# A fused attention, butterfly and linear-attention kernel: its semaphore waits rewritten, the instruction orders kept

## What is computed

```python
x = x + windowed_attention(_layernorm(x))    # 16 heads of 8, 2 key/value heads, window 32
x = x + butterfly_ffn(_layernorm(x))         # 128 -> 512, 9 butterfly stages, gelu, 9 stages, -> 128
x = x + linear_attention(_layernorm(x))      # elu+1 features, sum over all tokens of a batch
x = x + butterfly_ffn(_layernorm(x))
```

## Time and profile before

| | us |
|---|---|
| three executions | 560.13 (median), 557.11, 562.09 |
| span of the profiled execution | 560.6 |
| PE busy in it | 525.0 |
| DVE, POOL, ACT busy | 441.2, 450.9, 358.7 |

### The profile page before, as it was taken

How to read it: one execution, slowest core, us unless ns; L and a number is a source line. 1 busy time by engine, 2 the same in 40 slices (tenths; PEclk the granted TensorE clock), 3 DMA queues, 4 the chain that set the end, 5 groups by cost and what they waited for, 6 DMA issues and landing times. The chain is left out here.

```text
span 560.6 us, 14708 instructions
## 1 busy us (share of the span) xinstructions
PE 525.0 (94%) x5060; PEld 345.8 (62%) x5060; DVE 441.2 (79%) x1272; ACT 358.7 (64%) x578; POOL 450.9 (80%) x646
## 2 busy tenths in 40 slices
PE   5786998979999999999999999999999999999795
PEld 3442554546766666666667676666666667777563
DVE  5778789897888989898988898888989797663341
ACT  2543376567687767676777768686767777664532
POOL 6665689899898999999898989899999797955420
PEclk9789799989999999999999999999999999999899
DMA  9533232322223232232313231323232222100001
GB/s 310 170 76 81 63 83 54 81 74 56 54 58 80 62 76 66 68 78 48 102 45 87 63 87 44 84 60 77 61 76 50 59 66 58 39 1 20 1 20 37
DMA packets 49546, 38.88 MB, mean 69 GB/s; under 512 B 12352, under 2 KB 38976, under 8 KB 49472
## 3 DMA queue, kind: packets, MB, share of 16 engines
q1 hardware_dynamic: 47024, 33.73, 23.9%
q10 hardware_dynamic: 2448, 4.22, 2.1%
HBM read 15.64 MB, written 5.51 MB: 38 GB/s over the span
## 5 line engine op out<-in xcount | busy, mean ns | idle before, releaser
L501 POOL TENSOR_TENSOR probs_t<-probs_t,first 128x1024 f32<-128x1024 f32 x64 | 151.3, 2367 | 11.5 <-DMA probs_t<-probs_t 11.5
L645 PEld LDWEIGHTS ring<-w,early 128*128 128x128 f32 x1024 | 119.0, 192 | 9.6 <-issue 7.0
L982 ACT ACTIVATE early<-ring,b 128x512 f32<-128x512 f32 x128 | 87.2, 684 | 54.7 <-PE ring L633 53.1
L645 PE MATMUL ring<-w,early 128*128 128x128 f32 x1024 | 120.0, 275 | 0.8 <-ACT early L982 0.8
L972 ACT ACT_TABLE_LOAD x58 | 74.4, 1283 | 10.7 <-issue 9.7
L601 PE MATMUL ps_s<-kx,q_t 64*32 64x512 f32 x960 | 65.9, 606 | 3.4 <-DVE merged L1268 2.7
L633 PE MATMUL ring<-xT_G,w1b 128*128 128x512 f32 x128 | 67.1, 612 | 0.7 <-ACT xT_G L960 0.7
L991 ACT ACTIVATE probs_t<-merged_t 128x1024 f32<-128x1024 f32 x64 | 65.3, 1044 | 3.8 <-DVE merged_t L1275 3.7
L633 PE MATMUL ring<-xT_F,w1b 128*128 128x512 f32 x128 | 59.9, 611 | 0.4 <-ACT xT_F L960 0.4
L1255 DVE COPY_PREDICATED ps_s<-first,ps_s 128x512 f32<-128x512 uint32 x64 | 43.6, 681 | 9.2 <-PE ps_s L601 9.0
L1282 DVE STREAM_TRANSPOSE ps_o<-ps_o 128x512 f32<-128x512 f32 x64 | 46.2, 722 | 1.6 <-PE ps_o L618 0.3
(11 more groups left out here) (124 smaller groups left out, 1023.9 us busy)
## 6 DMA issues: line engine op xcount, KB each, us to landing
probs_t<-probs_t SPq DMA_DIRECT2D x256, 64.0 KB, 2.0
kx<-kv_rows SPq DMA_DIRECT2D x120, 40.0 KB, 2.2
x_P<-in_x SPq DMA_DIRECT2D x16, 256.0 KB, 3.2
out_x<-x_G SPq DMA_DIRECT2D x16, 256.0 KB, 2.4
vx_t<-kv_rows SPq DMA_DIRECT2D x128, 8.0 KB
up_s<-in_up_m ACTq DMA_DIRECT2D x7, 256.0 KB, 8.4
down_s<-in_down_m ACTq DMA_DIRECT2D x7, 256.0 KB, 8.4
kv_rows<-kv_t SPq DMA_DIRECT2D x16, 80.0 KB, 2.8
```

The costliest lines, as they stand in the source:

```text
L501: nc.gpsimd.tensor_tensor(parts, parts, keep.rearrange("p (a t) -> p a t", a=1).to_broadcast([P, PAIR * HEADS, WIN]), ALU.mult).then_inc(p ...
L645: last = nc.tensor.matmul(bank(name)[:, P * j:P * (j + 1)], hid[s][:, c, P * j:P * (j + 1)], w2[:, c], start=(c == 0), stop=(c == CH - 1))
L982: nc.scalar.activation(hid[s][:, c], bank(name)[:], ACT.Gelu, bias=b1[:, c:c + 1]).then_inc(drained[BANK[name]].sem, 1)
```

## The change

It rewrites the waits; what each engine does, and in which order, stays, but for six POOL instructions.

1. **Order of waits.** Wherever an operation has several waits, the one that is expected last is now written first, so that the operation itself carries it, and the early ones stand in the EVENT_SEMAPHORE.
2. **Two waits on one semaphore become one** (`both(...)`, the larger of the values). On ACT nearly every operation loses its EVENT_SEMAPHORE by this.
3. **`residual`** no longer ends with a wait for its own result; the wait stands at the head of `moments` instead. `head_outputs` and `linear_normalised` are split into one function per operation, called in the same order.
4. **POOL** drops `nm` and `nmr` where VectorE applies the norm itself (group 0 P, group 15 F and L), and the wait on the group before's `nmr`. The semaphore `pool_step` is called `rooted`.
5. **Bookkeeping.** The lags of all tables and turns are renumbered (`TURNS` from NG + 14 to NG + 7), runs of single pieces are put together; on PE, `W.PV0` now carries the wait on `parted` and `W.S0` the one on the keys' DMA.

The number of EVENT_SEMAPHORE instructions in the built program goes from 638 to 527 on DVE, from 355 to 79 on ACT, from 200 to 140 on POOL, from 248 to 251 on PE and from 65 to 63 on SP.

```diff
...
 class Count:
...
+    def both(self, *events):
+
+        return max(self.value(group, name) for group, name in events)
...
+            def rooted_variance(g, s, mean=None):
+                pool.wait_ge(vec.sem, vec.after(g, f"{s}.mv"))
+                nc.gpsimd.tensor_scalar(rv[s][:], mv[s][:, :, 1], LN_EPS, None, ALU.add).then_inc(rooted.sem, 1)
+                if mean is not None:
+                    nc.gpsimd.tensor_scalar(mean, mv[s][:, :, 0], -1.0, None, ALU.mult).then_inc(rooted.sem, 1)
+                pool.wait_ge(rooted.sem, rooted.after(g, f"{s}.rv"))
...
+                nc.gpsimd.tensor_tensor(rstd[s][:], rv[s][:], half[:], ALU.pow).then_inc(rooted.sem, 1)
+
             def normalise(g, s):
...
-                if (g == 0 and s == "P") or (g == NG - 1 and s in "FL"):
-                    return
+                rooted_variance(g, s, nm[s][:])
+                pool.wait_ge(rooted.sem, rooted.after(g, f"{s}.rstd"))
+                nc.gpsimd.tensor_tensor(nmr[s][:], nm[s][:], rstd[s][:], ALU.mult).then_inc(rooted.sem, 1)
+                pool.wait_ge(rooted.sem, rooted.after(g, f"{s}.nmr"))
                 pool.wait_ge(product.sem, product.after(g - 1, TURNED[s]))
-                pool.wait_ge(pool_step.sem, pool_step.after(g, f"{s}.nmr"))
...
             def copy_out(g, name, dst, *freed):
 
-                act.wait_ge(product.sem, product.after(g - 1, *freed))
-                act.wait_ge(product.sem, product.after(g, name))
+                act.wait_ge(product.sem, product.both((g, name), *((g - 1, user) for user in freed)))
...
             def probs_out(g, j):
                 ready(ACT.Exp)
 
+                act.wait_ge(vec.sem, vec.after(g, f"W.tr{j}"))
                 act.wait_ge(product.sem, product.after(g - 1, f"W.PV{j}"))
-                act.wait_ge(vec.sem, vec.after(g, f"W.tr{j}"))
...
             def residual(g, s, name, base):
 
+                dve.wait_ge(product.sem, product.after(g, name))
...
-                dve.wait_ge(biased.sem, biased.after(g, f"{base}.xb"))
-                dve.wait_ge(product.sem, product.after(g, name))
...
-                if s != "G":
-                    dve.wait_ge(own.sem, own.after(g, name))
...
             def row_max(g, j):
+                dve.wait_ge(vec.sem, vec.after(g, f"W.cp{j}"))
                 dve.wait_ge(drained["S"].sem, drained["S"].after(g - 1, f"W.S{j}"))
-                dve.wait_ge(vec.sem, vec.after(g, f"W.cp{j}"))
...
             def subtract_max(g, j):
-                dve.wait_ge(vec.sem, vec.after(g if j >= 2 else g - 1, f"W.tr{(j - 2) % 4}"))
-                dve.wait_ge(vec.sem, vec.after(g, f"W.max{j}"))
+                dve.wait_ge(vec.sem, vec.both((g, f"W.max{j}"), (g if j >= 2 else g - 1, f"W.tr{(j - 2) % 4}")))
...
```

More of the change, by code:

```diff
@@ L464, in add_bias @@
                         pool.wait_ge(bffn_made, 1)
-                behind = 2 if s == "P" else 1
-                pool.wait_ge(drained[BANK[used]].sem, drained[BANK[used]].after(g - behind, used))
                 if source is None:
@@ new lines, in turn @@
+                for g in due(t, 5):
+                    add_bias(g, "F", bproj_s, "F.down", "L.proj")
+                for g in due(t, 2, 2):
+                    add_bias(g, "P", bo_s, None, "W.proj")
+                for g in due(t, 4, 2):
+                    normalise(g, "W")
+                for g in due(t, 3, 0, 1):
+                    probs_parted(g, 2)
+                for g in due(t, 4, 0, 1):
+                    add_bias(g, "W", bffn_s, "W.proj", "F.down")
+                for g in due(t, 6, 0, 14):
+                    normalise(g, "L")
@@ new lines, in turn @@
+                for g in due(t, 3, 2):
+                    probs_parted(g, 2)
+                for g in due(t, 6):
+                    add_bias(g, "L", bffn_s, "L.proj", "G.down")
+                if t == 20:
+                    rooted_variance(15, "L")
+                for g in due(t, 4, 2):
+                    add_bias(g, "W", bffn_s, "W.proj", "F.down")
+                if t == 19:
+                    rooted_variance(15, "F")
+                for g in due(t, 3, 1):
+                    probs_parted(g, 3)
@@ L586, in scores @@
                 name = f"W.S{j}"
-                if j == 0:
-                    drained_by(g, "P.q", name)
-                    if g == 0:
-                        pe.wait_ge(early_cleared, 3)
-                        drained_by(0, "X.ka", name)
-                    else:
-                        pe.wait_ge(kx_in.sem, kx_in.after(g, "P.kx"))
-                if j == 2 and g == 0:
-                    drained_by(0, "X.kb", name)
+                if (name, "keys") not in COVERED and g > 0:
+                    pe.wait_ge(kx_in.sem, kx_in.after(g, "P.kx"))
+                drained_by(g, "P.q", name)
+                if g == 0:
+                    drained_by(0, "X.ka" if j < TPB else "X.kb", name)
+                    pe.wait_ge(early_cleared, 3)
                 free(g, name)
@@ L609, in weighted_values @@
                 name = f"W.PV{j}"
-                if j == 0:
+                pe.wait_ge(parted.sem, parted.after(g, f"W.um{j}"))
+                if (name, "values") not in COVERED:
                     pe.wait_ge(vec.sem, vec.after(g, "W.vx"))
-                pe.wait_ge(parted.sem, parted.after(g, f"W.um{j}"))
                 free(g, name)
@@ L779, in turn @@
-                for g in due(t, 7, 2, 15):
+                for g in due(t, 3, 2):
                     scores(g, 1)
+                if t == 5:
+                    weighted_values(1, 0)
+                    up_transposed()
+                    weighted_values(1, 1)
+                for g in due(t, 6):
+                    linear_kv_rows(g, 0)
+                    linear_q(g)
+                    linear_kv_rows(g, 1)
+                for g in due(t, 8, 0, 14):
+                    ffn_down(g, "G")
@@ new lines, in turn @@
+                for g in due(t, 5):
+                    norm_transposed(g, "F", "W")
+                for g in due(t, 3, 2):
+                    scores(g, 2)
+                for g in due(t, 4, 2):
+                    weighted_values(g, 1)
+                for g in due(t, 6):
+                    linear_state(g)
+                for g in due(t, 5):
+                    ffn_up(g, "F", 3)
+                    ffn_up(g, "F", 2)
+                    ffn_up(g, "F", 0)
+                    ffn_up(g, "F", 1)
@@ new lines, in turn @@
+                for g in due(t, 6, 0, 14):
+                    linear_out(g, 0)
+                for g in due(t, 7):
+                    norm_transposed(g, "G", "L")
+                if t == 21:
+                    linear_out(15, 0)
+                for g in due(t, 3, 1):
+                    scores(g, 3)
+                for g in due(t, 4):
+                    weighted_values(g, 2)
+                for g in due(t, 2, 2):
+                    attention_q(g)
+                for g in due(t, 5):
+                    ffn_down(g, "F")
@@ L791, in turn @@
-                for g in due(t, 10):
-                    linear_kv_rows(g, 0)
-                if t == 8:
+                    up_stage(3, "a")
+                    up_stage(3, "b")
+                    up_stage(4, "a")
+                    scores(0, 2)
+                    up_stage(5, "a")
+                    down_stage(1)
+                    scores(0, 3)
+                    attention_q(1)
+                    weighted_values(0, 0)
+                    down_stage(2)
+                    up_stage(4, "b")
@@ new lines, in turn @@
+                    scores(1, 0)
+                    up_stage(6, "a")
+                if t == 0:
+                    up_stage(2, "a")
+                    first_keys(1)
+                    scores(0, 0)
+                    norm_transposed(1, "P", "P")
+                    down_stage(0)
+                for g in due(t, 4, 0, 1):
+                    weighted_values(g, 3)
+                for g in due(t, 6, 0, 14):
+                    linear_out(g, 1)
+                for g in due(t, 7, 0, 14):
+                    ffn_up(g, "G", 3)
@@ new lines, in turn @@
+                if t == 21:
+                    linear_out(15, 1)
+                for g in due(t, 1, 2):
+                    norm_transposed(g, "P", "P")
+                if t == 4:
+                    heads_transposed(0)
+                if t == 3:
+                    down_stage(3)
+                    scores(1, 1)
+                    down_stage(4)
+                for g in due(t, 4, 2):
+                    weighted_values(g, 3)
+                for g in due(t, 2, 2):
+                    scores(g, 0)
@@ L934, in turn @@
-                if t == 27:
-                    ffn_up(15, "G", 3)
+                    up_stage(5, "b")
+                for g in due(t, 7):
+                    ffn_up(g, "G", 0)
+                if t == 22:
+                    ffn_up(15, "G", 3)
+                    ffn_up(15, "G", 2)
+                    ffn_down(15, "G")
```

(43 more changed lines are left out.)

684 lines of the change are left out of this document (254 added, 430 removed), and 77 rows, old and new, of tables (COVERED, PRODUCTS, VECTOR).

## The result

| | median us | executions | lowest to highest |
|---|---|---|---|
| before | 561.11 | 4 | 557.11 to 562.66 |
| after | 552.18 | 4 | 550.90 to 552.24 |

The ratio is 0.9843 (95% interval 0.9803 to 0.9883). A second round with six executions of the changed kernel gave 552.37, ratio 0.9862 (0.9836 to 0.9888).

A forecast was written before the change was run, and what follows sets the result against it. PE was taken to bound the middle, with chains of short dependent instructions stalling it in fill and drain. Savings of 2.3 and 1.3 us made 3.6 off 560.6, 557.0, then 556.6 as median; 8-in-10 range 552.5 to 560.0.

The forecast's parts named there:

- Bounds: Whole span: PE alone paces the middle; cheaper waits help only while the pipeline fills and drains.
- Another chain is just behind: Rival, in the fill: busy DVE and POOL or SP's key transfers hold the pace, only the drain gains; 558.8 us, chance 0.18.
- What one wait costs: Moving the late wait onto the operation saves 0.06 to 0.07 us on DVE, 0.10 on POOL, 0.06 on ACT.
- The fill and the drain: Waits on PE's critical chains at both ends of the span: 2.3 us saved in the fill, 1.3 in the drain.
- the sum: Whole kernel: 2.3 us in the fill plus 1.3 in the drain, 3.6 us off, giving 556.6.
- The clock pays back more: Rival, PE's half-clock stretches: two of the shorter ones vanish with shorter stalls, 3.4 us more off, 553.2 us; chance 0.13.
- the slower rival: Half-clock stretches fall into dense PE work: one more costs 3.4 us (560.0), two give 563.4; chance 0.06.
- The base: Starting time: 3.6 us off the profiled 560.6 us is 557.0; the median shown is 0.5 below that span, so 556.6.
- waits cost nothing: Rival, by the skill's rule: only POOL's 0.2 us twice and its `xn` waits count, 559.3 us; chance 0.10.
- DVE holds the whole fill: Rival, 25 to 125 us: nearly all 95 DVE waits count, 6.6 + 1.3 us off, 552.2 us; chance 0.08.

The follow-up runs named there:

- the 69 executions: The unchanged kernel before, run beside the experiments, two slow executions left out: 554.51 to 562.94 us, mean 559.5.
- POOL alone: Kernel before with only POOL's waits reordered, `nm` and `nmr` all kept: 557.61 us, ratio 0.9952.
- `nm` gone: Kernel before without the six needless `nm` and `nmr` instructions on POOL, waits otherwise as before: 558.25 us, ratio 0.9959.
- DVE alone: Kernel before with only DVE's waits reordered and merged: 555.26 us, ratio 0.9911.
- ACT alone: Kernel before with only ACT's waits merged and reordered: 558.47 us, ratio 0.9970.
- the three together: Kernel before with the waits of DVE, ACT and POOL rewritten, `nm` and `nmr` kept, PE's and SP's waits as before: 553.89 us, ratio 0.9893.
- The kernel with the longer stall: Changed kernel plus one needless ACT activation ahead of the key copies, PE's stall before the first scores 3.05 instead of 2.57 us: 554.21 us, ratio 0.9904.

## Why the prediction was wrong

**Bounds.** Right. Nothing but PE paced the middle (30.24 before, 30.23 after), and the gain lies in the fill and in the drain. That DVE and POOL are 85 to 90% busy in the fill was read too broadly from the earlier trace rows: it holds for 94 to 125 us (92% and 90%), while from 25 to 57 us they are at 81% and 55%. The rival "Another chain is just behind" leaned on it.

**What one wait costs.** Right for DVE (0.10 to 0.04 measured) and in kind for POOL, where the saving is 0.07 and not 0.10. For ACT the 0.06 taken from DVE is what the drain shows: four stalls behind a copy or gelu went from 0.36, 0.75, 0.75 and 0.84 to 0.30, 0.69, 0.69 and 0.78. The Trainium skill's sentence ("VectorE: DVE Perf Modes", section "The DRAIN you can't avoid") that the semaphore between DVE operations costs nothing extra does not hold for a wait in an instruction of its own: 0.10 against 0.04 us in the rows, and the kernel with DVE's waits alone is 0.9911 of before.

**The fill and the drain.** The drain's stalls were right within 0.02 us: those of 3.08, 0.34 and 1.50 us shrank by 0.49, 0.07 and 0.43 where 0.48, 0.07 and 0.41 were written, and the four behind ACT by 0.06 each. (The stall of 3.08 us is before group 14's `o_l`, not group 15's as the prediction has it; the sum does not depend on it.) The fill has no such clean reading, because the clock moved with it. What is left of the rest, 3.3 - 1.3 = 2.0, stands against the 2.3 of the sum. With the slope of 0.84 instead of 1 the clock's 4.2 us become 3.5, and the rest of the mean gain of 7.4 is 3.9. So the change without the clock is worth 3.3 to 3.9 us, and the 3.6 lies in between.

**The step that failed** is the clock. The sum left the dips of the profiled execution where they were, and "they simply begin earlier" was said of PE stretches whose lengths do change when the clock does. The rival "The clock pays back more" had the mechanism, but was mis-sized twice. It let two short dips go, 3.4 us off with a chance of 0.13; three went in the profile, two of them of 6.8 us, and the mean loss fell by 4.2 us, worth 3.5 to 4.2 in time. And its counter-argument, "the stalls shrink by tenths of 2 to 3 us", looked at each stall's size alone. The runs say that what PE idles in all goes with the loss, and that 3.0 to 4.4 us less of it (32.1 to 29.1 and 27.7) came with 4.2 us less of clock loss. The three times shown of before were a sign I read only for the slower rival: 5 us of spread with one program is clock, as the 69 executions show, and so the clock was open to both sides.

**The base** was a smaller error. I set the profiled span against the median, 0.5 apart. In the 69 executions the device time is 1.8 to 2.0 us above the span, so that execution took some 562.5 us, at a clock of 0.978, at the slow end. From the mean of before, 559.5, the sum gives 555.9; less 3.5 to 4.2 of clock this is 551.7 to 552.4.

**The slower rival** did not come about: no edit raised the loss above before's. "Another chain" and "waits cost nothing" fall with DVE's 2.2 us of rest. "DVE holds the whole fill" named 552.2, which is the measured time, by luck and for a wrong reason: DVE's waits alone stop at 555.3.

**Still open** is which stall is followed by a dip in one execution. The same program has stretches at half clock in other places from run to run (the changed kernel from 115 and 514 us in one profile, from 18 and 53 us in the other). The stall before the first scores is 2.72 to 2.79 us in the profiles of six kernels; a stretch of 6.8 us comes with it in two (before, POOL alone), one of 3.4 us in two (`nm` gone, DVE alone) and none in two (ACT alone, the three together). The kernel with the longer stall also speaks against one stall deciding alone.

## What to carry to other kernels

Write the wait that comes last first, so that the operation carries it, and fold waits on one semaphore into one: on a chain of short dependent steps that is 0.06 to 0.07 us a step here, and nothing where the engine that sets the pace does not wait. When PE stalls in short pieces, count the granted clock as a second term: split each execution into clock loss and rest before a profile is set against a median, since shorter stalls can save a second time through the clock, here about as much as they saved themselves. A cheap test is to fill a stall with idle products into a bank that is free when the stall begins.

## What was not expected of the hardware

- Idle products made the kernel faster: three of them in a stall of 2.8 us took the mean clock loss from 8.5 to 5.3 us and the median from 560.36 to 556.89.
- One program's time moves by 8 us (554.51 to 562.94) with its mean granted clock (0.994 to 0.979), in stretches at half clock that last 3.4 or 6.8 us.
- On POOL a directly carried wait costs 0.07 to 0.08 us behind `rstd` but 0.11 in front of `xn`; why these differ was not tried.
